# Decoder kernel: position biases and norm sums moved between VectorE and GpSimd, key masks and start-up constants moved

## The reference

```
x = x + L0_attn(x)            # causal attention with 4 "future" columns, then norm, GELU perceptron
x = x + L0_xattn(norm(x), ctx, mask)   # 375 keys + 64 memory keys, 16 heads of 16
x = x + L0_ffn(norm(x))       # mixture of 8 experts, top 2, and a shared perceptron
x = x + L1_attn(norm(x))      # offset attention, below
x = x + L1_xattn(norm(x), ctx)         # causal cross attention
x = x + L1_ffn(norm(x))       # quantised gated perceptron
```

```
lg = (q . k[o back]) / sqrt(16) * (1 + q . scale_embed[o]) + pos_bias[o]     # -1e30 for other offsets
p = softmax(lg);  out = sum_o p[o] * v[o back] * if_gain * sigmoid(x @ gate_w.T + gate_b)
```

## Time and profile before

| | us |
|---|---|
| median of 3 runs (lowest, highest) | 1950.75 (1946.47, 1958.93) |
| the profiled execution's own time | 1952.74 |
| its span, first to last instruction | 1951.1 |
| PE busy in the span | 1739.1 (89%) |
| DVE, ACT, POOL busy | 883.5, 863.6, 411.2 |
| mean granted TensorE clock, share of full speed | 0.939 |

### The profile page before, as it was taken

The page is one execution under the profiler, slowest core; times in us unless marked ns, Lnnn a source line. Parts: engine busy times, 40 slices in busy tenths (PEclk is TensorE's granted clock), DMA queues, the critical chain, the costliest instruction groups (busy, mean ns, idle before and its releaser), DMA issues. The chain is left out here.

```text
span 1951.1 us, 34080 instructions
## 1 busy us (share of the span) xinstructions
PE 1739.1 (89%) x13418; PEld 1145.6 (59%) x13418; DVE 883.5 (45%) x1418; ACT 863.6 (44%) x1779; POOL 411.2 (21%) x351
## 2 busy tenths in 40 slices
PE   7899999789899999999869899999896987799965
PEld 3455555545366666656654899996343665466642
DVE  4555656241455555555422211111553645266637
ACT  4243434323355555555511222222344877255556
POOL 0011112161100000000015500004333756101112
PEclk9999999799899999999959899999897999799968
DMA  6000000100200000000012999993178331000001
GB/s 232 1 1 1 1 1 1 33 17 0 75 16 10 17 17 9 17 17 2 2 60 73 333 334 325 326 323 116 29 196 205 84 76 42 19 11 11 1 1 38
DMA packets 147915, 150.08 MB, mean 77 GB/s; under 512 B 69760, under 2 KB 134976, under 8 KB 147760
## 3 DMA queue, kind: packets, MB, share of 16 engines
q1 hardware_dynamic: 144544, 139.82, 23.3%
q0 software_dynamic: 3216, 8.11, 1.4%
HBM read 120.39 MB, written 27.53 MB: 76 GB/s over the span
## 5 line engine op out<-in xcount | busy, mean ns | idle before, releaser
L1049 DVE TENSOR_REDUCE x_negmax<-psum 112x2 f32<-112x878 f32 x128 | 131.2, 1067 | 89.7 <-PE psum L878 89.7
L891 PEld LDWEIGHTS psum<-ident,x_probs 112*125 112x125 f32 (+1 forms) x1024 | 118.3, 170 | 75.4 <-issue 47.0
L891 PE MATMUL psum<-ident,x_probs 112*125 112x112 f32 (+1 forms) x1024 | 140.7, 276 | 15.9 <-DVE x_turned L1055 15.3
L988 ACT ACTIVATE x_probs<-psum,x_negmax 112x439 f32<-112x439 f32 x256 | 146.6, 629 | 17.0 <-DVE x_negmax L1049 17.0
L2105 DVE TENSOR_TENSOR masked<-masked 128x512 f32<-128x512 f32 x70 | 49.7, 710 | 207.2 <-ACT masked L2088 207.2
L2058 PE MATMUL psum<-experts_xb,experts_up 128*128 128x128 f32 x1120 | 133.0, 278 | 6.2 <-DMA experts_down<-in_moe_down 6.2
L2058 PEld LDWEIGHTS psum<-experts_xb,experts_up 128*128 128x128 f32 x1120 | 132.7, 195 | 8.1 <-DMA experts_down<-in_moe_down 6.4
L994 ACT COPY x_turned<-psum 125x448 f32<-125x448 f32 x128 | 68.0, 531 | 146.3 <-PE psum L891 145.5
L2066 PE MATMUL psum<-experts_down,masked 128*128 128x256 f32 x560 | 126.8, 380 | 0.1
L1350 PE MATMUL psum<-fold_full,hT 128*112 128x512 f32 x256 | 113.8, 598 | 1.3 <-DVE fold_part L1628 1.3
L2066 PEld LDWEIGHTS psum<-experts_down,masked 128*128 128x128 f32 x560 | 103.7, 190 | 12.9 <-issue 0.3
(11 more groups left out here) (320 smaller groups left out, 3446.7 us busy)
## 6 DMA issues: line engine op xcount, KB each, us to landing
experts_up<-in_moe_up SPq DMA_DIRECT2D x35, 1024.0 KB, 5.8
experts_down<-in_moe_down SPq DMA_DIRECT2D x35, 1024.0 KB, 7.9
offset_rows<-prep_rows SPq DMA_DIRECT2D x16, 784.0 KB, 6.3
a_factor<-offset_rows SPq DMA_DIRECT2D x16, 784.0 KB, 5.4
x_ctx<-in_ctxT SPq DMA_DIRECT2D x16, 375.0 KB, 3.2
slots_x<-zeros SPq DMA_DIRECT2D x1, 4480.0 KB, 21.1
experts_rows<-slots_x SPq DMA_DIRECT2D x35, 128.0 KB, 2.8
slots_y<-experts_result SPq DMA_DIRECT2D x35, 128.0 KB, 3.1
```

Source lines behind the costliest of these rows:

```text
L891: mm = nc.tensor.transpose(psum[0:CHUNK_ROWS[c], 4 + i % 2, k * T:(k + 1) * T], probs[:, n % 2, slot_of_head(HG * g + k), c * CHUNK:c * CH ...
L988: nc.scalar.activation(probs[:, n % 2, slot], psum[0:T, slot % 4, 0:KEYS], ACT.Exp, bias=negmax[:, n % 2, slot:slot + 1]).then_inc(exped.s ...
L1049: nc.vector.tensor_reduce(negmax[:, n % 2, 2 * pair:2 * pair + 2], psum[0:T, b:b + 2, 0:KEYS], X, ALU.max, negate=True).then_inc(maxed.sem, 1)
```

## The change

Start-up: ln1 is loaded after the tokens of group 1, on a semaphore of its own, ACT waits for that one in `affine` and for no constants before. ln2 and rank count on another semaphore; VectorE still waits for all but ln1 before its casts.

GELU perceptron: the flags are loaded from the SP queue at the stage's start. The mask is written by VectorE, a quarter in each group, between the norm's scaling and the addition to the residual. POOL has none of it.

Offset attention: VectorE adds the biases of r = 0 and 1, POOL those of 2 and 3, and the order of multiplications is 0, 2, 1, 3. The norm's first sum and sum of squares go from POOL to VectorE, the sum of squares from iteration 7, 11, 15 to 8, 12, 16. The centring goes in front of `largest` 2 and 3.

```
+    def dve_sum(self, dve, n):
+        for norm, g in self.sums(n):
+            norm.sum_halves(dve, g, norm.nc.vector)
+    def dve_pair(self, dve, n):
+        for norm, g, half in self.halves(n - 1):
+            if half == 0:
+                norm.sum_squares(dve, g, norm.nc.vector)
...
         def affine(g):
             act.wait_ge(s["normed"], g + 1)
+            act.wait_ge(affine_loaded.sem, affine_loaded.n)
...
         @block.sync          # gelu_perceptron
         def _(sp):
+            load_flags(sp)
             next_weights.load(sp)
...
                 norm.centre(dve, other, 6)
                 norm.scale(dve, other)
+                mask_keys(dve, g)
                 dve.wait_ge(*hidden_read.after(n, M8 - 1))
...
-                if g == 0:
-                    mask_keys(pool)
...
-                    pe.wait_ge(*banks_free.after(At(n - 1), r))
+                    pe.wait_ge(*banks_free.after(At(n - 1), (0, 2, 1, 3)[r] if offset else r))
...
+            def add_bias_here(n, r):
+                dve.wait_ge(*factored.after(At(n), 2 * r))
+                x = probs[:, n % 2, HG * r:HG * (r + 1)]
+                nc.vector.tensor_tensor(x, x, bias[:, HG * r:HG * (r + 1)], ALU.add).then_inc(biased_here.sem, 1)
...
-                    dve.wait_ge(*biased.after(At(n), r))
+                    dve.wait_ge(*(biased_here.after(At(n), r) if r < 2 else biased.after(At(n), r - 2)))
...
                 if now and offset:
-                    for r in range(NG):
-                        multiply(n, r)
-                    for r in range(NG):
-                        largest(n, r)
+                    multiply(n, 0)
+                    multiply(n, 2)
+                    add_bias_here(n, 0)
+                    multiply(n, 1)
+                    largest(n, 0)
+                    multiply(n, 3)
+                    add_bias_here(n, 1)
+                    beside.dve_pair(dve, n)
+                    largest(n, 1)
                     beside.dve_centre(dve, n, 6)
+                    largest(n, 2)
+                    largest(n, 3)
                     take_values(n)
+                elif offset:
+                    beside.dve_pair(dve, n)
...
                 beside.dve_scale(dve, n)
+                if offset and beside.sums(n):
+                    dve.wait_ge(*added.after(At(n - 2)))
+                    beside.dve_sum(dve, n)
...
                 if n < NB and offset:
-                    add_bias(n, 0)
-                    add_bias(n, 1)
+                    add_bias(n, 2)
                 if n >= 2:
                     normalise(n - 2)
                 if n < NB and offset:
-                    add_bias(n, 2)
                     add_bias(n, 3)
...
-                beside.pool_pair(pool, n)
-                if n and beside.sums(n):
+                if not offset:
+                    beside.pool_pair(pool, n)
+                if n and beside.sums(n) and not offset:
...
             def start_sp(sp):
                 first.load(sp, a["xT"], 0)
                 folded.load(sp)
-                for g in range(1, GROUPS):
+                first.load(sp, a["xT"], 1)
+                affine_loaded.inc(sp.dma_start(ln1[:], a["ln1"]), 16)
+                for g in range(2, GROUPS):
                     first.load(sp, a["xT"], g)
...
                 first.dve(dve)
-                dve.wait_ge(loaded.sem, 16 * 7)
+                dve.wait_ge(late_loaded.sem, 16 * 2)
+                dve.wait_ge(loaded.sem, 16 * 4)
...
                 act.wait_ge(made.sem, 6)
-                act.wait_ge(loaded.sem, 16 * 7)
-                first.act(act)
+                first.act(act, affine_loaded)
...
+            def mask_keys(dve, g):
+                some = slice(g * BATCHES_OF, (g + 1) * BATCHES_OF)
+                keys = masked[:].rearrange("p (b s) -> p b s", b=NB)[:, some]
+                dve.wait_ge(flags_loaded.sem, 16)
+                nc.vector.memset(keys[:, :, S2:KEYS], 0.0)
+                nc.vector.tensor_scalar(keys[:, :, 0:S2], flags[:].bitcast(U8).rearrange("p (b s) -> p b s", b=NB)[:, some], NEG, None, ALU.mult)
```

More of the change, by code:

```diff
@@ L442, in dve, with act @@
         f.copy_even(dve, (14,))
-    def act(self, act):
+    def act(self, act, affine_loaded):
         nc, s, f = self.nc, self.sig, self.f
@@ L606, in _, with gelu_perceptron @@
                 nc.vector.tensor_tensor(dst[:, :, t], dst[:, :, t], sq[:, g, 1].unsqueeze(1).broadcast_to([P, C, G]), ALU.mult).then_inc(ns.normed, 1)
-def gelu_perceptron(nc, psum, w, hT, accT, yT, beside, next_weights, mask_keys):
+def gelu_perceptron(nc, psum, w, hT, accT, yT, beside, next_weights, load_flags, mask_keys):
     up, down = w.at["up"], w.at["down"]
@@ L1260, in token_attention @@
             factor_loaded = s.loads("factor_loaded", 1)
-            factored, biased, gated = s.counter("factored", NG), s.counter("biased", NG), s.counter("gated", 1)
+            factored, biased, biased_here, gated = s.counter("factored", NG), s.counter("biased", 2), s.counter("biased_here", 2), s.counter("gated", 1)
         if future:
@@ L1580, in _ @@
         def _(dve):
-            for x in (q_read, maxed, shifted, added) + ((v_read,) if not future else (qk_made, fscored, fmaxed, combined, centred, fsummed, fmixed)) + ((factored,) if offset else ()):
+            for x in (q_read, maxed, shifted, added) + ((v_read,) if not future else (qk_made, fscored, fmaxed, combined, centred, fsummed, fmixed)) + ((factored, biased_here) if offset else ()):
                 x.start(dve)
@@ L1740, in add_bias @@
             def add_bias(n, r):
-                pool.wait_ge(*factored.after(At(n), r))
+                pool.wait_ge(*factored.after(At(n), 2 * r - 3))
                 x = probs[:, n % 2, HG * r:HG * (r + 1)]
@@ L2564, in decoder @@
         const = {"ident": ident, "spreader": spreader, "identb": identb, "maskb": maskb, "ones_row": ones_row, "masked": masked, "round": rnd, "one": one, "half": half, "rank": rank, "plan": a["plan"]}
-        loaded, made, cast = (Chain(nc.alloc_semaphore(x)) for x in ("constants_loaded", "constants_made", "constants_cast"))
+        loaded, affine_loaded, late_loaded, made, cast = (
+            Chain(nc.alloc_semaphore(x)) for x in ("constants_loaded", "first_affine_loaded", "late_constants_loaded", "constants_made", "constants_cast"))
         zeroed = Chain(nc.alloc_semaphore("slots_zeroed"))
@@ L2618, in start_sp @@
                 folded.load(sp)
-                for g in range(1, GROUPS):
+                first.load(sp, a["xT"], 1)
+                affine_loaded.inc(sp.dma_start(ln1[:], a["ln1"]), 16)
+                for g in range(2, GROUPS):
                     first.load(sp, a["xT"], g)
-                for dst, src in ((ln1[:], a["ln1"]), (ident[:], a["ident"]), (maskf[:], a["causal"]), (half[:], a["half"]), (spreader[:], a["spreader"])):
+                for dst, src in ((ident[:], a["ident"]), (maskf[:], a["causal"]), (half[:], a["half"]), (spreader[:], a["spreader"])):
                     loaded.inc(sp.dma_start(dst, src), 16)
@@ L2624, in start_sp @@
                 for dst, src in ((ln2[:], a["ln2"]), (rank[:], a["rank"])):
-                    loaded.inc(sp.dma_start(dst, src), 16)
+                    late_loaded.inc(sp.dma_start(dst, src), 16)
                 f0.load(sp)
@@ L2655, in decoder, with load_flags @@
                             startup={"sp": start_sp, "dve": start_dve, "pe": start_pe, "act": start_act}, big=big, spare=masked[:].bitcast(F32))
-            masks, flags_loaded = Chain(nc.alloc_semaphore("masks")), Chain(nc.alloc_semaphore("flags_loaded"))
+            flags_loaded = Chain(nc.alloc_semaphore("flags_loaded"))
             flags = sb_f("flags", [P, NB * S2 // 4], U32)
-            def mask_keys(pool):
-                flags_loaded.inc(pool.dma_start(flags[:], a["mask"].broadcast_to([P, NB * S2 // 4])), 16)
-                masks.inc(nc.gpsimd.memset(masked[:], 0.0))
-                pool.wait_ge(masks.sem, masks.n)
-                pool.wait_ge(flags_loaded.sem, flags_loaded.n)
-                nc.gpsimd.tensor_scalar(masked[:].rearrange("p (b s) -> p b s", b=NB)[:, :, 0:S2], flags[:].bitcast(U8).rearrange("p (b s) -> p b s", b=NB), NEG, None, ALU.mult)
-            gelu_perceptron(nc, psum, f0, hT, xT, yT, Beside(n2, n3), x0, mask_keys)
+            def load_flags(sp):
+                flags_loaded.inc(sp.dma_start(flags[:], a["mask"].broadcast_to([P, NB * S2 // 4])), 16)
+            def mask_keys(dve, g):
[4 more added lines that the diff above has]
+                nc.vector.tensor_scalar(keys[:, :, 0:S2], flags[:].bitcast(U8).rearrange("p (b s) -> p b s", b=NB)[:, some], NEG, None, ALU.mult)
+            gelu_perceptron(nc, psum, f0, hT, xT, yT, Beside(n2, n3), x0, load_flags, mask_keys)
         memory_attention(nc, psum, const, x0, hT, xT, a["ctxT"], Beside(n3, n4), shared)
```

## The result

The changed kernel takes **1922.99 us** (median of 4 runs, 1919.49 to 1929.67), against 1954.78 for the kernel before in the same rounds (4 runs, 1946.47 to 1958.93). The ratio is 0.985, 95% interval 0.982 to 0.988, so some 30 us. The profiled execution took 1922.52 with a span of 1920.7. Between the two profiles the span is 30.4 us shorter, where the sum had 22.5.

The account below looks back on a forecast made before the run. TensorE, busy for 89% of the span, was taken as the bound. The terms -6.0 - 10.1 + 1.0 - 8.4 + 1.0 = -22.5 us took the profiled 1952.74 to 1930.2, 1928 as a median; range 1914 to 1941.

Parts of the forecast that it names:

- Start-up (-6.0): Start-up: ScalarE's square no longer waits for the last constant; variance 5.6 to 6.1 us earlier, carried to the end as -6.0.
- Perceptron (-10.1 + 1.0): Perceptron: group 1's round becomes like group 2's, -10.1 us; VectorE's mask work before the stage's end costs +1.0.
- Offset norm iterations (3 x -3.8 and 3 x +1.0): Offset attention, three norm iterations: earlier centring gains 3.8 us each, low clock costs about 1.0 each; together -8.4.
- the clock's 1.0 a group: Offset norm iterations: the new wait may put TensorE at its low clock again, about 1.0 us each.
- the wait at some 2 us: Offset norm iterations: TensorE waits some 2 us for VectorE's sum of squares before the variance product, in place of 0.63.
- Ordinary iterations (0): Offset attention without a norm: VectorE's added biases just fit, so 0 us, ends -2 and +7.
- the very first (+1.0): Offset attention's first iteration: nothing hides VectorE's biases, so later maxima come about 1 us later for ScalarE, +1.0.
- The shared port: VectorE beside GpSimd: two trace lines disagree; the skill's rule that the second comer is fully blocked was kept as a rival.
- rival D: Offset attention: VectorE's biases and GpSimd's work hold each other, +38 us over 12 iterations; sum +16, 1967 us; 5%.
- B: Offset norm iterations: the variance's new wait drops the clock and ScalarE's queue ends them; stage gives 0, median 1936; 20%.
- E: Start-up: its wait was not on the constants, or another late load takes its place; -16, 1936 us; 2%.
- C: More gained, clock and waits both go: -14 offset, -7 start-up, -10 perceptron; 1922 by profile, 1920 as median; 18%.

Follow-up runs that it names:

- experiment 3: Changed kernel with the start-up's loads and waits put back as before: 1929.95 us, ratio 0.9881 to the kernel before.
- experiments 1 and 2: Kernel before with only the mask moved to VectorE in quarters: ratio 0.9948; changed kernel with the mask on GpSimd in quarters: ratio 0.9851.
- the mask in quarters: Changed kernel with the mask back on GpSimd, in quarters behind each group's sums: 1923.78 us, ratio 0.9851.
- changed kernel's second profile: The changed kernel itself, unaltered, timed and profiled once more: 1924.89 us, ratio 0.9852 to the kernel before.
- experiment 8: Changed kernel with the norm's sum of squares back on GpSimd, first sum still on VectorE: 1921.80 us, ratio 0.9842.
- experiment 9: Changed kernel with the sum of squares back on GpSimd and the norm's scaling in front of the output's addition: 1917.90 us, ratio 0.9815.

## Why the prediction was right, and where its sizes were off

The forecast was 1928 us and the median 1922.99. Each of the three parts gained by the cause that was named for it; the sum fell short by 7.9 us for the reasons below.

**Start-up (-6.0).** The steps came as described; 4 to 7 us by experiment 3, and at the first projection 5.6 in the mean of all profiles. The variance product came 6.28 us earlier.

**Perceptron (-10.1 + 1.0).** The hold by the mask was the cause (experiments 1 and 2). A quarter of the mask takes VectorE 0.88 us, below the lowest of the three rows that I priced it from (1.05). The last addition starts 104.99 us into the stage, where the shorter round alone would put it at 104.7, so the term is about 0.3, not 1.0.

**Offset norm iterations (3 x -3.8 and 3 x +1.0).** The cause was right, and the size of -3.8 about so: the first group gave 4.77, the second 3.70 (27.18 to 23.48), the third and the drain 3.09, together 11.56 where 11.4 was worked out before the clock's price. That the three come so near 11.4 in sum is partly luck, since the last has the clock's price in it. **The term that failed is the clock's 1.0 a group**, in the first two groups. The new wait of 2.83 us was there, and what followed ran at full speed. (I had put the wait at some 2 us; the numbers of that paragraph give 4.5 - 2.43 + 0.63 = 2.7.) In the third group TensorE did run at the lower level, after another wait: 1.87 us for ScalarE, then the output product in 3.73 us. With the mask in quarters, the same code ran that product in 2.01 and the drain in 33.31 us, not 35.70. It is not a term without substance, though: in the kernel with the start-up undone, whose code is the same here, the same wait of 2.83 us was followed by the lower of the two levels (1.2 GHz), at which the product took 1.83 us in place of 0.99. Timeline of that kernel:

```profile
1562.47 1.83 PE L273 MATMUL psum<-sq,averager 128*128 128x448 f32 x2 [2.83 <-DVE sq L269]
1564.09 0.95 PE L1387 MATMUL psum<-ident,a_probs 112*112 112x112 f32 x4
```

and of the changed kernel's second profile:

```profile
1558.12 0.99 PE L273 MATMUL psum<-sq,averager 128*128 128x448 f32 x2 [2.83 <-DVE sq L269]
1558.95 0.55 PE L1388 MATMUL psum<-ident,a_probs 112*112 112x112 f32 x4
```

The stretches behind the wait say the same in the granted clock, 0.72 and 1.00 (columns as in the earlier trace rows). First the one with the start-up undone:

```profile
1557.50:1567.00 9.50, 6.67 (x61) 4.02 (x56) 5.49 (x11) 4.03 (x11) 1.45 (x1) 0.72 0.37 86
```

and the changed kernel again:

```profile
1557.20:1566.00 8.80, 7.31 (x97) 5.42 (x98) 3.91 (x9) 6.11 (x18) 2.97 (x3) 1.00 0.40 93
```

Iteration 8 took 15.44 us in the one, 13.63 in the other, and iteration 12 15.19 and 13.64: 1.8 and 1.55. Four kernels have this code, with two such groups each: in six the clock cost nothing, or 0.3 us at most, and in two it cost 1.8 and 1.55, both in one execution. 1.0 fits neither. What decides between them stays open.

**Ordinary iterations (0) and the very first (+1.0).** Over the nine ordinary ones the gain was 0.5 us. ScalarE's wait of 0.42 us for the third maximum went, and the iterations of 8.54 became 8.38. The first two grew by 0.10, not 1.0: the first took 5.77 us where it had 6.07, and in all kernels with the multiplications in the order 0, 1, 2, 3 it stayed at 6.07 or 6.08.

**What the sum missed.** 3.2 in the norm groups (11.56 for 8.4), which is mostly the clock's price that two of them didn't pay, 0.9 of the first iteration, 0.5 of ordinary ones, 0.8 in the perceptron, 0.5 in the start-up, and 2.1 in stages that the change doesn't touch. The last is no effect: the same stretch took 262.0 to 265.0 us in the kernels above. Together, before rounding, that is the 7.9 between -22.5 and -30.4.

**The shared port was misjudged.** From one row I took it that a VectorE operation with two SBUF inputs is not blocked by GpSimd. Three kinds of rows here say it is. L285 ends 0.94 us behind the gate that it came 0.10 after, and takes 1.08 when it comes first. GpSimd's first bias takes longer when it starts just behind VectorE's, here in iteration 4 of the changed kernel, both biases of GpSimd:

```profile
1515.35 0.62 DVE L1627 TENSOR_TENSOR a_probs<-a_probs,weights 112x448 f32<-112x448 f32 x1
1515.51 1.46 POOL L1770 TENSOR_TENSOR a_probs<-a_probs,weights 112x448 f32<-112x448 f32 x1 [1.80 <-DVE a_probs L1622]
...
1519.46 1.14 POOL L1770 TENSOR_TENSOR a_probs<-a_probs,weights 112x448 f32<-112x448 f32 x1
```

And with the sum of squares on GpSimd (experiment 8), VectorE's second bias comes second and takes 1.06:

```profile
1555.10 1.14 POOL L1767 TENSOR_TENSOR a_probs<-a_probs,weights 112x448 f32<-112x448 f32 x1
...
1555.65 1.06 DVE L1627 TENSOR_TENSOR a_probs<-a_probs,weights 112x448 f32<-112x448 f32 x1
```

The Trainium skill (SBUF — State Buffer, Who interferes with whom) says of such operations that the second is blocked until the first is done, and these rows bear it out in both directions, but for the 0.1 to 0.2 us by which the second ends sooner than its own length behind the first; the row of 1.27 us beside 1.97 does not fit it. It isn't the only one: in the changed kernel the same VectorE product came in the middle of the same GpSimd conversion and was hardly held at all, 0.74 us where its median is 0.69.

```profile
1088.43 1.97 POOL L2238 TENSOR_SCALAR rounded_weights<-raw_weights 128x704 bf16<-128x704 f32 x1
1089.01 0.74 DVE L2131 TENSOR_TENSOR masked<-masked 128x512 f32<-128x512 f32 x1 [5.03 <-ACT masked L2114]
```

So beside this conversion the hold is not for its whole length, and no run here says why. What kept rival D away is the order that its paragraph names: in all 32 biases of VectorE in the changed kernel the duration is 0.61 to 0.62, and in no case does one start while a GpSimd instruction runs, and GpSimd's 0.3 us of hold lie where nobody waits.

**The other rivals.** B would have needed iteration 8 to eat the gain; it ate 2.04 of 6.81 us, 1.67 of them by the sum of squares on VectorE (experiment 8). E is out by the earlier trace rows and the row at 9.17. C came nearest in the total (1920), and by its mechanism in part: no output product waited for the centring, and in the first two groups no clock was lost; in the drain it was.

## What to carry to other kernels

When a wait names a short instruction, look at what stands ahead of it in that engine's own queue: here moving one line past two waiting maxima gave 14.55 us in a stage, while 38 instructions moved to a less busy engine, with the wait left in place, gave 0.9, which is less than the drain of one code varies by. A step moved to the emptier engine is only earlier if it isn't put behind that engine's own burst. And the clock's price behind a wait of a given length comes whole in some executions and not at all in others, so put both into the range rather than half into the sum.

## What the runs showed of the hardware that was not expected

- GpSimd wants 4.01 us for 128x1500 flags from uint8 to bf16, VectorE 0.88: a factor of 4.6, while for an f32 addition of 128x448 it is 1.14 to 0.62, 1.8.
- The 0.9 us for which GpSimd's gate held the scaling moved the first multiplication of iteration 9 by 1.1, and the end of iteration 10 by 0.1: iterations 8 to 10 together are 30.07 us with it (experiment 8) and 29.95 without (experiment 9).
- The same code, up to the perceptron, differed by 8.7 us between profiles (372.21 to 380.91), and in the one pair looked at closely nearly all of it came from the last stretch. The two with the first projection at 47.55 and 47.85 us, the changed kernel and the one with the mask's quarters on GpSimd, began the perceptron at 376.19 and 372.21. Their granted clock was 0.99 to 1.00 in every stretch of 20 us from 210 to 350 us; from there to the perceptron it was 0.69 over 26.2 us in the one and 0.81 over 22.2 in the other. The shares not granted, 0.31 of 26.2 and 0.19 of 22.2, come to 8.1 and 4.2 us, about the difference of 4.
- The drain of the offset stage does the same on a smaller scale: 33.31 to 35.70 us in four kernels with the same code there, with the output product at 2.01 us in the shortest and 3.73 in the changed kernel's.
